# Values of a transformer layer projected in three chunks of 88 tokens a half, and moved to the sequences' partitions within SBUF

## What is computed

```python
for i in range(L):                                    # L = 4
    nx = t5_layer_norm(h, ln1[i])
    q = (nx @ attn_q[i]).reshape(b, s, H, DK)          # H = 12, DK = 64, F = H * DK = 768
    k = (nx @ attn_k[i]).reshape(b, s, H, DK)
    v = (nx @ attn_v[i]).reshape(b, s, H, DK)
    scores = jnp.einsum('bqhd,bkhd->bhqk', q, k) + bias
    attn = jax.nn.softmax(scores, axis=-1)
    ctx = jnp.einsum('bhqk,bkhd->bqhd', attn, v).reshape(b, s, H * DK)
    h = h + ctx @ attn_o[i]
    nx = t5_layer_norm(h, ln2[i])
    y = jax.nn.relu(nx @ ffn_wi[i]) @ ffn_wo[i]
    if i in MOE_LAYERS:                                # layers 1 and 3
        y = y + moe_ffn(nx.reshape(-1, d), gate_w[mi], moe_w1[mi], moe_w2[mi]).reshape(b, s, d)
        mi += 1
    h = h + y
```

## Time and profile before

| what | us |
|---|---|
| three runs | 820.2, 820.5, 829.17 |
| median | 820.5 |
| the profiled execution | 820.7 |
| its span in the trace | 818.9 |

### The profile page before, as it was taken

One profiled execution on the slowest core, in us unless ns is written; L12 is line 12 of the kernel. 1 busy time (PEld: TensorE's weight loads), 2 busy tenths in 40 slices (PEclk: granted clock), 3 DMA queues, 4 the chain that ended last, 5 costly groups with the idle time before them and its releaser, 6 DMA issues.

```text
span 818.9 us, 16360 instructions
## 1 busy us (share of the span) xinstructions
PE 751.7 (92%) x6708; PEld 666.5 (81%) x6735; DVE 439.7 (54%) x917; ACT 407.4 (50%) x913; POOL 352.6 (43%) x326
## 2 busy tenths in 40 slices
PE   7977999888998998999999999998989999999996
PEld 4764578777886987889899988778879788999995
DVE  0347524356355475556566635654453955666664
ACT  1476433353355334376777535434454444866742
POOL 3356414364547442045676244444453501544430
PEclk9987896898999798999999999989997999999998
DMA  7221000020312201033444230003112010533300
GB/s 198 78 68 40 2 2 30 0 79 2 106 30 68 68 3 54 2 121 107 138 124 125 61 78 1 2 3 105 38 61 68 1 55 7 155 96 106 98 1 21
DMA packets 36610, 49.21 MB, mean 60 GB/s; under 512 B 6155, under 2 KB 27575, under 8 KB 36023
## 3 DMA queue, kind: packets, MB, share of 16 engines
q1 hardware_dynamic: 33259, 43.49, 18.6%
q10 hardware_dynamic: 3276, 4.67, 1.8%
HBM read 47.70 MB, written 0.45 MB: 59 GB/s over the span
## 4 chain that ended last, share of the span: by engine, by line
PE 66%; DVE 12%; ACT 11%; POOL 5%; issue 3%; DMA 2%; SPq 0%; POOLq 0%; ACTq 0%; DVEq 0%
PE pd L651 36%; PE pa L651 20%; PE ps L651 8%; POOL w L580 3%; PE pa L682 3%; ACT wide L1013 2%; ACT wqkv L925 1%; DVE prob L1206 1%; DVE mx L1053 1%; POOL prob L589 1%; ACT pa L1014 1%; DVE hT L1133 1%; DVE rc L1058 1%; DVE xn L1093 1%; DVE xs L1063 1%
## 5 line engine op out<-in xcount | busy, mean ns | idle before, releaser
L580 POOL TENSOR_TENSOR w<-raw,w 128x384 fp32r<-128x384 f32 x140 | 142.7, 1021 | 125.9 <-ACT w L925 118.1
L651 PE MATMUL pd<-wide,w 128*128 128x264 f32 x1200 | 162.4, 294 | 0.0
L651 PEld LDWEIGHTS pd<-wide,w 128*128 128x128 f32 x1200 | 156.1, 197 | 1.0 <-DVE wide L1229 0.4
L651 PE MATMUL pa<-xs,w 128*128 128x264 f32 x810 | 122.6, 291 | 11.4 <-DVE wide L1229 6.4
L651 PEld LDWEIGHTS pa<-xs,w 128*128 128x128 f32 x810 | 107.9, 191 | 16.8 <-DVE wide L1229 8.4
L589 POOL TENSOR_TENSOR prob<-prob,mx 66x792 f32<-66x792 f32 x36 | 54.9, 1528 | 86.5 <-DVE mx L1053 86.3
L1229 DVE TENSOR_TENSOR wide<-pa,wide 128x264 fp32r<-128x264 f32 x144 | 61.4, 430 | 33.7 <-ACT pa L1014 31.7
L651 PE MATMUL ps<-xs,w 128*128 128x264 f32 x480 | 74.5, 285 | 2.4 <-DVE prob L1206 2.4
L651 PE MATMUL pa<-wqkv,xs 128*66 128x384 f32 x320 | 72.0, 371 | 1.5 <-ACT vtok L997 1.5
L1013 ACT ACTIVATE wide<-pa 128x264 fp32r<-128x264 f32 x144 | 56.7, 394 | 33.5 <-PE pa L651 33.3
L601 POOL TENSOR_TENSOR rs<-var,exponent 88x3 f32<-88x3 f32 x22 | 18.6, 848 | 123.7 <-DVE var L1075 123.7
(11 more groups left out here) (120 smaller groups left out, 1250.9 us busy)
## 6 DMA issues: line engine op xcount, KB each, us to landing
raw<-in_moe_w_dram SPq DMA_DIRECT2D x16, 576.0 KB, 4.1
raw<-in_moe_w_dram SPq DMA_DIRECT2D x16, 384.0 KB, 3.4
raw<-in_moe_w_dram SPq DMA_DIRECT2D x32, 192.0 KB, 3.9
vtok<-cw_rows ACTq DMA_DIRECT2D x4, 1056.0 KB, 6.1
raw<-in_attn_o_dram SPq DMA_DIRECT2D x4, 576.0 KB, 4.0
raw<-in_ffn_wo_dram SPq DMA_DIRECT2D x4, 576.0 KB, 4.0
vtok<-in_patches_dram SPq DMA_DIRECT2D x2, 768.0 KB, 7.9
raw<-in_attn_q_dram SPq DMA_DIRECT2D x4, 384.0 KB, 3.8
```

Source lines behind the costliest of these rows:

```text
L580: ins = nc.gpsimd.tensor_tensor(low, whole, high.bitcast(F32), ALU.subtract)
L651: return nc.tensor.matmul(out_ap, lhsT, rhs, start=first, stop=last)
```

## The change

A half's values are projected in three chunks of 88 tokens (3 x 88 = 264) instead of four sequences of 66. A chunk has again two groups of five matmuls with 384 moving columns; only the stationary operand has 88 columns instead of 66. `v` of b = 3 falls away. ScalarE copies the two groups of a chunk to a new tile `v_rows` of the half, which lies in the memory of `wide` of that half. It then waits until its own two copies are done and issues two DMAs from SBUF to SBUF, which bring the rows of the chunk to partitions 0 to 65 of the sequences they belong to (`V_MOVES`: 66 and 22 rows, 44 and 44, 22 and 66, each row 3072 bytes). TensorE's first `pv` of a half waits for the semaphore `v_moved` of that half instead of the last copy.

```diff
+VC, VCN = 3, NT // 3
+V_MOVES = (((0, 0, 0, S), (1, 0, S, VCN - S)),
+           ((1, VCN - S, 0, 2 * S - VCN), (2, 0, 2 * S - VCN, 2 * VCN - 2 * S)),
+           ((2, 2 * VCN - 2 * S, 0, 3 * S - 2 * VCN), (3, 0, 3 * S - 2 * VCN, S)))
...
-                yield ("v", 0, layer, b)
+                if b < VC:
+                    yield ("v", 0, layer, b)
...
+        with nc.sbuf_tensor("w1_place", [128, 4 * F], F32), \
+                nc.sbuf_tensor("v_rows0", [VCN, VC, F], F32) as v_rows0, \
+                nc.sbuf_tensor("v_gap", [128, 2 * KT * NT - VC * F], F32), \
+                nc.sbuf_tensor("v_rows1", [VCN, VC, F], F32) as v_rows1:
+            pass
+        v_rows = [v_rows0, v_rows1]
...
                 elif name == "v":
-                    b = stage[3]
+                    c = stage[3]
                     pe.wait_ge(chunk_split, chunks_until("qkv", stage[2], 2))
                     for n in range(2):
                         cols = slice(n * F // 2, (n + 1) * F // 2)
-                        tok = slice(b * S, (b + 1) * S)
+                        tok = slice(c * VCN, (c + 1) * VCN)
                         pairs = split_pairs(wqkv[:, 0, 2], wqkv[:, 1, 2], xs[hf][:, :, tok], cols)
-                        product(bank_a()[0:S, 0:F // 2], [(x, w) for w, x in pairs], a_full)
+                        product(bank_a()[0:VCN, 0:F // 2], [(x, w) for w, x in pairs], a_full)
...
                     if b == 0:
-                        pe.wait_ge(a_free, groups_after(A_GROUPS, ("v", hf, layer, HALF_B - 1)))
+                        pe.wait_ge(v_moved[hf], 16 * 2 * VC * (layer + 1))
...
                     for n in range(2):
-                        nc.scalar.activation(vtok[0:S, hf * HALF_B + b, n * F // 2:(n + 1) * F // 2], bank_a()[0:S, 0:F // 2],
+                        nc.scalar.activation(v_rows[hf][:, c, n * F // 2:(n + 1) * F // 2], bank_a()[0:VCN, 0:F // 2],
                                              ACT.Copy).then_inc(a_free, 1)
+                    act.wait_ge(a_free, groups_after(A_GROUPS, stage))
+                    for b, to, at, rows in V_MOVES[c]:
+                        act.dma_start(vtok[to:to + rows, hf * HALF_B + b, :], v_rows[hf][at:at + rows, c, :]).then_inc(v_moved[hf], 16)
```

More of the change, by code:

```diff
@@ L185, in stages @@
                 yield ("scores", 1, layer, b)
-                yield ("v", 1, layer, b)
+                if b < VC:
+                    yield ("v", 1, layer, b)
             yield from o(0, layer)
@@ L413, in vit_tower @@
         h1_ready = sem("h1_ready")
+        v_moved = [sem("v_moved0"), sem("v_moved1")]
         sq_ready, rs_ready, x_ready = sem("sq_ready"), sem("rs_ready"), sem("x_ready")
@@ L914, in high_part @@
                 if kind == "qkv" and layer:
-                    act.wait_ge(a_full, groups_after(A_GROUPS, ("v", 1, layer - 1, HALF_B - 1)))
+                    act.wait_ge(a_full, groups_after(A_GROUPS, ("v", 1, layer - 1, VC - 1)))
                 elif kind == "o" and layer:
@@ L991, in _ @@
                 elif name == "v":
-                    layer, b = stage[2:4]
-                    if b == 0 and layer - 1 in MOE_LAYERS:
+                    layer, c = stage[2:4]
+                    if c == 0 and layer - 1 in MOE_LAYERS:
                         act.wait_ge(d_free, groups_after(D_GROUPS, ("y_main", hf, layer - 1, EXPERTS)))
                     for n in range(2):
-                        nc.scalar.activation(vtok[0:S, hf * HALF_B + b, n * F // 2:(n + 1) * F // 2], bank_a()[0:S, 0:F // 2],
+                        nc.scalar.activation(v_rows[hf][:, c, n * F // 2:(n + 1) * F // 2], bank_a()[0:VCN, 0:F // 2],
                                              ACT.Copy).then_inc(a_free, 1)
+                    act.wait_ge(a_free, groups_after(A_GROUPS, stage))
+                    for b, to, at, rows in V_MOVES[c]:
+                        act.dma_start(vtok[to:to + rows, hf * HALF_B + b, :], v_rows[hf][at:at + rows, c, :]).then_inc(v_moved[hf], 16)
                 elif name == "pv":
```

## The result

| | us | mean granted clock |
|---|---|---|
| before, median of 4 runs | 820.95 | |
| changed, median of 4 runs (830.49 to 835.28) | 832.8 | 0.908 |
| ratio, with its 95% interval | 1.0211 (1.0154 to 1.0268) | |
| the profiled execution of the changed kernel | 835.28 | 0.902 |
| its span | 833.5 | |

The forecast was 821.6 us, with 814 to 829 as its range. The ratios, here and in the experiments, are taken over the faster runs of each kernel alone (those within some 1.5% of its fastest) and so are not the quotients of the medians; that would be 1.014 here.

What follows compares the result with a forecast made beforehand. TensorE was taken as the bound on the whole, but at seven of eight places other engines release the work behind the removed block. 820.7 - 1.9 (places) + 3.0 (clock) = 821.8, against the median 821.6 us; range 814 to 829.

Steps and rivals of the forecast that it cites:

- The work removed: Value projection, all eight halves: three blocks of 1.97 us replace four of 1.88; ceiling 12.9 us saved.
- What each place is worth at an unchanged clock: Gains and losses at the eight value projections (four layers, two halves), summed without clock changes: -1.9 us.
- L2h0: Layer 2, half 0: fourth block comes off the path, less ScalarE's lateness and wider blocks; -1.2 us.
- L0h1 and L2h1: Layers 0 and 2, half 1: first half of the fourth block goes, wider blocks give back 0.15; -0.85 us each.
- L1h1: Layer 1, half 1: wider blocks +0.4 us; bank rotation frees the first transposes of a wait, -1.1.
- L3h1: Layer 3, half 1: wider blocks +0.1 us; bank rotation makes the first transposes wait, +1.1.
- L0h0: Layer 0, half 0: fourth block hides behind VectorE, wider blocks cost at half clock; +0.5 us, gap near 4.
- The pair of issues: Two DMA issues on ScalarE behind each chunk's copies: between 0.7 and 1.5 us, taken as 0.9 with the wait.
- L1h0 and L3h0: Layers 1 and 3, half 0: nothing gained, hidden tiles come out even; bounds -0.8 and +0.6 us.
- Rival three: The move itself: a pair of issues costs 1.5 us and landing takes 6.1; 826 us, chance 0.13.
- The clock: Longer TensorE gaps lower its clock: two falls of 1.5 us reach the chain's end; +3.0 us, between -6 and +10.5.
- Rival two: Each of seven longer TensorE gaps brings a clock fall of 1.5 us on the dense work behind; 829 us, chance 0.20.

Runs made afterwards that it cites:

- e2_nomove: Changed kernel without the 48 DMAs: ScalarE copies each chunk straight into `vtok`, rows not regrouped by sequence; 835.4 us, 1.0128 of the kernel before.
- e11_change: The changed kernel run again, unaltered, on another group's chip; 832.9 us, 1.0253 of the kernel before.
- e9_sp_warm_all: Changed kernel with SyncE issuing the DMAs, eight fillers before hidden tiles (layers 1, 3), four before half 0's output projection (layers 0, 2); 812.7 us, ratio 0.9994.
- e6_dense_sp: Kernel before with three chunks in layers 0 and 2 only, DMAs issued by SyncE; 826.7 us, 1.0095 of the kernel before.
- e14_sp_warm_again: Changed kernel with SyncE issuing the DMAs and eight fillers ahead of the hidden tiles in layers 1 and 3, a repeat; 816.2 us, ratio 0.9975.

## Why the prediction was wrong, point by point

**The work removed: right in kind, a little small.** I took 1.97 us for a block, since weight columns seemed to be paid in full. It takes 1.90 (239.01 to 240.91), 0.190 per matmul against 0.188 with 66 weight columns. By the Trainium skill (TensorE: Matmul & The Clock Gate, Step-by-step) the next weights load beside the running matmul and the wider load would be free; the trace is nearer to that than to my 0.197. So my reading of 0.188 as the price of all 450 columns did not hold. The ceiling was about 8 x (7.52 - 5.70) = 14.6 us, and e2_nomove did 12 us less work at full clock, about 8 when set right for its lower clock.

**What each place is worth at an unchanged clock: mostly right in kind, the sum too small.** Over all, e11_change does 10 us less work at full clock than the kernel before, about 6 when set right for the lower clock (an estimate), where I had 1.9. L2h0 gave its 1.2 us (`qk` of L2h1: the layer's start was 1.4 later than before, this 0.2), but with luck: the scores of b = 3 wait 1.82 instead of 0.67 us, 1.15 more where I had 0.55, and low stretches at different places (on the first value block before, on the fillers now) hid it. The output projections of L0h1 and L2h1 wait 1.32 instead of 0.31. In L1h1 the first transposes wait no more and in L3h1 they do, 1.32 us, as the rotation said. L0h0 I had at +0.5, with a gap near 4; the gap is 1.85 and `qk` came 4.2 us earlier, as the clock was full over part of the value blocks there and low over `qk` (9.33 us instead of 7.54):

```profile
151.27 1.03 PE L666 MATMUL pa<-xs,wqkv 128*128 128x264 f32 x3 [1.85 <-DVE xs L1083]
```

**The pair of issues: the step that was mis-sized.** "a pair costs between 0.7 and 1.5, and I take 0.9 with the wait". It costs 1.6, above my upper bound:

```profile
L1016 ACTq DMA_DIRECT2D vtok<-v_rows x48: 757/770/1382, 131.8 to 652.6; - x48
```

(minimum, median and maximum in ns). I had put the bound at two issues of 0.74 and then chosen the value of an issue of quite another shape, and "ScalarE gains two copies of 0.48 us and loses the 0.9 of a pair, so the hidden tiles, which it paces, come out even" was followed only to the hidden tiles on ScalarE, not to the weight split behind the pair and to GpSimd behind that. At L1h0 and L3h0 that adds 1.2 us of wait. Rival three had a dearer pair, 1.5 us, at +0.6 a place and not through the weight split; its other part, a wait for the landing, did not come: no transposes wait for a DMA.

**The clock: the step that failed.** "I count two falls that reach the end of the chain, 3.0 us." The mean added part rose by 19 us (57 to 76.5), beyond my bound of 10.5. The price of 1.5 us a fall was read from one value block; a fall lasts longer than a block. The low stretch at 599 to 606 covers five hidden tiles, the first of 1.44 us instead of 0.84. L3h1 is low from 657 to 664 and again from 667 to 674, the second time behind another wait, the 1.32 us ahead of the transposes. The waits, too, became longer than the "from about 1 to 3" that I had written: 4.25, 2.76, 4.29 and 3.40 us. Rival two, the clock, named the gaps and the sign and got 0.20; it should have been the forecast. Its size was 829.1, from seven falls at 1.5.

The row that spoke against it (full clock after 2.05 us of waiting at 155.44) was one place in one execution. The same `qk`, behind 3.80 us of waiting, began at the low level in e9_sp_warm_all and took 8.97 us instead of 7.54. For waits of 1.3 to 2.63 us it differed between places and executions whether a fall came; for those of 2.76 us and more ahead of the hidden tiles one came each time, 24 of 24. One place in one execution could not tell this. The Trainium skill's rule on waits between bursts (TensorE: Matmul & The Clock Gate, HAM oscillation) is borne out: waits of 4.25, 2.76, 4.29 and 3.40 us ahead of the hidden tiles all came with a low clock, as did 3.10 in e2_nomove.

**What would have shown it.** "The forecast is wrong if [...] the low stretches of the clock change by more than 6 us in all": low time is 2 x 818.9 x 0.068 = 111 us before and 2 x 833.5 x 0.098 = 163 after.

What stays open: why one and the same place falls in one run and not in the next, how the lost clock divides over the layers (e6_dense_sp), and how the 12 us of the issuer divide over the places.

## What to carry to other kernels

Where TensorE waits for other engines behind the work that is removed, removing it can do worse than gain nothing: here the wait grew, the clock fell, and the dense work behind ran at half speed. Count such waits, price them from the length of a low stretch (3 to 10 us here) and not from one block, and fill them, with other stages or with fillers. A DMA issue is an instruction of the issuing engine: give it to an engine on which nothing is queued that others wait for, and follow what is queued behind it through every engine.

## What the hardware showed that I had not expected

- An issue of an SBUF-to-SBUF DMA of 22 to 66 rows of 3072 bytes takes 0.77 us whoever issues it: 757/770/1382 ns on ScalarE, and on SyncE in e14_sp_warm_again:

```profile
L553 SPq DMA_DIRECT2D vtok<-v_rows x48: 734/764/1519, 131.7 to 644.7; - x48
```

The number of rows hardly matters; the six issues of layer 1, half 0 (two each of 22, 44 and 66 rows), changed kernel:

```profile
L1016 ACTq DMA_DIRECT2D vtok<-v_rows x6: 757/770/789, 241.5 to 253.0; - x6
```

The Trainium skill (DMA: Bandwidth & Descriptors, Issuing engines are not separate DMA queues) calls the sequencer's time "usually small relative to the DMA itself". Here it is not small: a pair took 1.6 us of the issuer, and the 264 KB of the first pair of layer 1, half 0 were carried in the 2.6 us from 242.4 to 245.0 (104 GB/s in that stretch). With eight fillers, moving the issuer was worth 10 to 12 us.

- The saving shows as work at full clock and not in the time. The figure falls with the clock, though: 750 to 752 us against 762 without fillers, at a clock of 0.90 to 0.91, but 755 to 757 with SyncE and fillers, at 0.92 to 0.93.
- Fillers that do no work made the kernel with three chunks faster by 0.9 to 1.5% (ScalarE as issuer: 1.0104 and 1.0119 against 1.0211 and 1.0253) and the kernel before not at all (1.0044).
